# Masked attention over 4096 nodes on one core: the scores of a pair as seven half-size products instead of eight

## What is computed

```python
h = relu(layernorm(x))                     # x: 4096 x 512
q, k, v = h @ W_q.T + b_q, h @ W_k.T + b_k, h @ W_v.T + b_v
z = (q @ k.T) / sqrt(512)                  # 4096 x 4096
z = z * adj                                # adj: 0 or 1, 4096 x 4096
z = where(z == 0, -10000, z)
out = x + relu(softmax(z, axis=1) @ v)
```

## Time and profile before

| | us |
|---|---|
| median of 3 runs | 1589.69 (1583.79 to 1591.4) |
| the profiled execution | 1589.79 |
| its span | 1588.0 |
| PE busy, share of span | 1559.6, 98% |
| DVE busy | 1121.8, 71% |
| ACT busy | 554.0, 35% |
| transfers | 254.20 MB, mean 160 GB/s |

### The profile page before, as it was taken

The page is one execution under the profiler, slowest core; times in us unless marked ns, Lnnn a source line. Parts: engine busy times, 40 slices in busy tenths (PEclk is TensorE's granted clock), DMA queues, the critical chain, the costliest instruction groups (busy, mean ns, idle before and its releaser), DMA issues.

```text
span 1588.0 us, 18704 instructions
## 1 busy us (share of the span) xinstructions
PE 1559.6 (98%) x7246; PEld 721.8 (45%) x7246; DVE 1121.8 (71%) x1306; ACT 554.0 (35%) x666; POOL 2.3 (0%) x11
## 2 busy tenths in 40 slices
PE   7899999899999999999999999999999999999998
PEld 3344444344444444444444444444444444444444
DVE  5766764478776877687767776777767776777675
ACT  1233332243334333433334332433343333333342
POOL 0000000000000000000000000000000000000000
PEclk9899999999999999999999999999999999999999
DMA  4344325464544554455345533554435543453241
GB/s 165 120 145 160 133 106 184 162 227 171 184 160 153 182 184 158 159 186 187 145 158 185 206 142 144 185 192 173 142 143 211 186 153 128 171 199 120 67 160 67
DMA packets 75320, 254.20 MB, mean 160 GB/s; under 512 B 8288, under 2 KB 8288, under 8 KB 73440
## 3 DMA queue, kind: packets, MB, share of 16 engines
q1 hardware_dynamic: 75232, 253.00, 44.5%
HBM read 220.47 MB, written 32.51 MB: 159 GB/s over the span
## 4 chain that ended last, share of the span: by engine, by line
PE 95%; DVE 2%; issue 0%; ACT 0%; DVEq 0%; ACTq 0%
PE z L437 42%; PE o L452 42%; PE o L398 5%; PE o L412 5%; PE o L380 1%; PE z L483 0%; PE z L464 0%; PE z L474 0%; DVE o_rows L863 0%; DVE dot_waste L752 0%; DVE slots L885 0%; DVE stats L711 0%; DVE slots L790 0%; DVE run_min L802 0%; DVE acc L744 0%
## 5 line engine op out<-in xcount | busy, mean ns | idle before, releaser
L437 PE MATMUL z<-h_buf,g_buf 128*128 128x512 f16 x3072 | 683.8, 379 | 0.0
L452 PE MATMUL o<-v_buf,p_hi 128*128 128x512 f16 x2048 | 610.1, 380 | 0.4 <-issue 0.4
L437 PEld LDWEIGHTS z<-h_buf,g_buf 128*128 128x128 f16 x3072 | 300.7, 98 | 362.6 <-issue 1.1
L452 PE MATMUL o<-v_buf,p_lo 128*128 128x512 f16 x1024 | 388.6, 379 | 0.0
L785 DVE TENSOR_TENSOR slots<-slots,adj_buf 128x512 f32<-128x512 f32 x256 | 176.2, 691 | 283.4 <-ACT slots L592 283.2
L598 ACT ACTIVATE slots<-slots,log_p 128x1024 f32<-128x1024 f32 x128 | 147.2, 1150 | 474.4 <-DVE slots L822 474.4
L452 PEld LDWEIGHTS o<-v_buf,p_hi 128*128 128x128 f16 x2048 | 200.7, 98 | 237.9 <-issue 2.1
L592 ACT ACTIVATE slots<-z,c_all,kappa 128x512 f32<-128x512 f32 x256 | 198.9, 777 | 289.8 <-PE z L437 263.9
L829 DVE TENSOR_TENSOR p_lo<-slots,p_hi 128x1024 f16<-128x1024 f32 x128 | 156.6, 1224 | 45.0 <-PE o L452 30.0
L822 DVE TENSOR_TENSOR slots<-slots,floor_b 128x1024 f32<-128x1024 f32 x128 | 155.3, 1219 | 13.8 <-ACT floor_b L611 10.3
L790 DVE SCALAR_TENSOR_TENSOR slots<-slots 128x1024 f32<-128x1024 f32 x128 | 156.6, 1223 | 3.7
(11 more groups left out here) (89 smaller groups left out, 378.4 us busy)
## 6 DMA issues: line engine op xcount, KB each, us to landing
adj_buf<-in_adj SPq DMA_DIRECT2D x128, 512.0 KB, 5.6
v_buf<-v_dram SPq DMA_DIRECT2D x128, 512.0 KB, 3.7
g_buf<-g_dram SPq DMA_DIRECT2D x112, 512.0 KB, 4.6
x_rows<-in_x SPq DMA_DIRECT2D x12, 1024.0 KB, 8.0
v_dram<-v_buf SPq DMA_DIRECT2D x16, 512.0 KB, 7.5
g_dram<-g_buf SPq DMA_DIRECT2D x16, 512.0 KB, 8.0
h_dram<-h_buf SPq DMA_DIRECT2D x7, 1024.0 KB, 6.5
h_buf<-h_dram SPq DMA_DIRECT2D x7, 1024.0 KB, 8.2
```

What stands on the lines that cost most here:

```text
L437: mm = pe.matmul(z_bank[i % 2][t][:, :], g_buf[:, i % G_BUFS, a, k, t * P:(t + 1) * P], h[:, b, k, :], start=(k == 0 and m == 0), stop=(k ...
L452: mm = pe.matmul(o_bank[t][:, :], a[:, kt, span], v_buf[:, n % V_BUFS, kt, b, :], start=(j == 0 and kt == 0 and m == 0), stop=(j == PAIRS ...
```

## The change

- **Seven products.** `scores(i, piece)` splits the folded keys of a pair into 2 x 2 blocks (two key tiles by two halves of the contraction) and the block of h into 2 x 2 (two halves of the contraction by two halves of the queries). The four blocks of the scores come from seven block products (the Strassen scheme in Winograd's form) instead of eight. Each product has 2 chunks x 3 = 6 matmuls of 128x256, so a step has 42 of 128x256 where it had 24 of 128x512.
- **Sums.** The key-side sums S1 to S4 are made once, in the opening stage (`combine_g`), and stored beside the keys: a pair of g has seven operands (`OPS`) instead of four chunk pairs, 896 KB instead of 512 KB for each load. The query-side sums T1 to T4 are made for every block (`combine_t`, `high_t`, `low_t`), in steps 7 to 12 of the block two before.
- **PSUM.** Products are added in the banks `za0`/`za1`, `zb`, `zd`, and read out between products: ACT makes seven copies of 128x256 per step instead of two of 128x512. TensorE's pieces wait for these (`m1_copied`, `u2_copied`, `m7_copied`, `u4_copied`, and the next pair for `m2_copied`, `d_copied`, `c12_copied`). DVE adds the copies (`add_c11`, `add_c2`); `weigh` is one instruction of 128x1024 instead of two.
- **Order.** In the main loop the pieces of `scores` stand between the four `weigh_v`. `LEAD` is 19 and there are 20 slots; g and v have 3 buffers instead of 4.
- **Opening.** `normalise` moves from DVE to ACT, DVE does the sums and splits seven operands. The next chunk of folded keys waits only for ACT's copy to `g_stage` (`g_copied`). Three pairs of the second block, instead of two, are scored ahead of step 0.
- Bias and x are handled in other steps, x comes back in halves, and several buffers share memory.

```diff
-        g_buf = sb("g_buf", [P, G_BUFS, 2, KC, 2 * P], F16)
+        g_buf = sb("g_buf", [P, G_BUFS, 2, OPS, 2, P], F16)
...
+            def product(i, bank, op, right, fresh):
+                for j in range(2):
+                    for m, (a, b) in enumerate(HI_LO):
+                        mm = pe.matmul(bank[:, 0:QH], g_of(i)[:, a, op, j, :], right[b][j],
+                                       start=(fresh and j == 0 and m == 0), stop=(j == 1 and m == 2),
+                                       skip_group_check=not fresh)
+                return mm
...
+                    product(i, a, A11, of_h(s, 0, 0), True).then_inc(za_ready, 1)
+                    if i >= 1:
+                        pe.wait_ge(m2_copied, i)
+                    product(i, b_bank, A12, of_h(s, 1, 0), True).then_inc(zb_ready, 1)
+                if piece == 1:
+                    if j == 0:
+                        pe.wait_ge(t_lo_ready, KC * (s + 1))
+                    pe.wait_ge(m1_copied, i + 1)
+                    product(i, a, S2, of_t(s, T2), False).then_inc(za_ready, 1)
+                    if i >= 1:
+                        pe.wait_ge(d_copied, i)
+                    product(i, d_bank, S3, of_t(s, T3), True).then_inc(zd_ready, 1)
+                if piece == 2:
+                    pe.wait_ge(u2_copied, i + 1)
+                    product(i, a, S1, of_t(s, T1), False).then_inc(za_ready, 1)
+                    pe.wait_ge(m7_copied, i + 1)
+                    product(i, d_bank, A22, of_t(s, T4), False).then_inc(zd_ready, 1)
+                if piece == 3:
+                    pe.wait_ge(u4_copied, i + 1)
+                    product(i, a, S4, of_h(s, 1, 1), False).then_inc(za_ready, 1)
...
+            def copy_u2(i):
+                act.wait_ge(za_ready, 4 * i + 2)
+                if i >= 1:
+                    act.wait_ge(c2_added, i)
+                nc.scalar.activation(um_tmp[:, 0, :], a_bank[i % 2][:, 0:QH], ACT.Identity, bias=key_term(i, 1),
+                                     scale=kappa[:, 0:1]).then_inc(u2_copied, 1)
...
+            def low_g(q, j):
+                for u in range(2):
+                    g = g_of(2 * q + u)
+                    dve.wait_ge(g_hi_ready, 4 * q + 2 * j + u + 1)
+                    v.tensor_tensor(g[:, 1, :, j, :], g_stage[:, 0:OPS, u, :], g[:, 0, :, j, :], ALU.subtract
+                                    ).then_inc(g_lo_ready, 1)
...
+            def add_c2(i):
...
+                v.tensor_tensor(slot(i)[:, 1, :], um_tmp[:, :, :].rearrange("p a n -> p (a n)"),
+                                dm_tmp[:, :, :].rearrange("p a n -> p (a n)"), ALU.add).then_inc(c2_added, 1)
```

More of the change, by code:

```diff
@@ L658, in _ @@
[L658 to L667 removed]
+            normalise(4)
@@ new lines, in _ @@
+            for n in range(-3, STEPS):
+                s, j = n // PAIRS, n % PAIRS
+                first = j == PAIRS - 2 and 0 < s + 1 < BLOCKS
+                more = n + LEAD < STEPS
+                soon = 2 <= n + 2 < STEPS
+                if PAIRS <= n + LEAD - 1 < STEPS:
+                    copy_c12(n + LEAD - 1)
+                if j == 0 and s >= 1:
+                    copy_o(s - 1, 3)
+                if more:
+                    copy_m1(n + LEAD)
+                    copy_m2(n + LEAD)
+                if soon and not first:
+                    exp(n + 2)
+                if more:
+                    copy_u2(n + LEAD)
+                    copy_m7(n + LEAD)
+                if first:
+                    copy_floor(s + 1, a_bank[0])
+                if n == -1:
+                    copy_floor(0, o_bank[3])
+                if soon and not first:
+                    high_p(n + 2)
+                if s >= 0 and s + 2 < BLOCKS:
+                    if j == 9:
+                        high_t(s + 2, 0)
+                    if j == 10:
+                        high_t(s + 2, 1)
+                        high_t(s + 2, 2)
+                    if j == 11:
+                        high_t(s + 2, 3)
+                if more:
+                    copy_u4(n + LEAD)
+                    copy_d(n + LEAD)
+                if n == -1:
+                    exp(0)
+                    high_p(0)
+                    exp(1)
+                    high_p(1)
+                if first:
@@ new lines, in _ @@
+            add_c11(PAIRS)
+            add_c2(PAIRS)
+            halve_min(0)
+            weigh(PAIRS)
+            add_c11(PAIRS + 1)
+            negate(PAIRS)
+            see_min(PAIRS)
+            add_c2(PAIRS + 1)
+            columns_min(0, o_bank[2])
+            weigh(PAIRS + 1)
+            add_c11(PAIRS + 2)
+            negate(PAIRS + 1)
+            lower(0)
+            add_c2(PAIRS + 2)
+            lower(1)
+            see_min(PAIRS + 1)
+            low_p(0)
+            for n in range(STEPS):
+                s, j = n // PAIRS, n % PAIRS
+                first = j == PAIRS - 2 and s + 1 < BLOCKS
@@ L988, in _ @@
                 i = n + LEAD
-                if n + 2 < STEPS and not first:
+                more, scored = i < STEPS, i - 1 < STEPS
+                if first:
+                    halve_min(s + 1)
+                elif n + 2 < STEPS:
                     lower(n + 2)
-                if 0 <= n + 1 < STEPS:
+                if scored:
+                    weigh(i - 1)
+                if n + 1 < STEPS:
                     low_p(n + 1)
-                    add_up(n + 1)
-                if first:
-                    halve_min(s)
@@ L1011, in _ @@
-                if j == 0 and s >= 1:
-                    halve_acc(s - 1)
+                if j == PAIRS - 1:
+                    row_gain(s)
+                if first:
+                    columns_min(s + 1, a_bank[0])
+                if scored:
+                    negate(i - 1)
+                if n + 1 < STEPS:
+                    add_up(n + 1)
+                if j == PAIRS - 2:
+                    halve_acc(s)
+                if more:
+                    add_c11(i)
+                if s >= 1 and j in (1, 3):
+                    add_bias(s - 1, j - 1, j + 1)
```

910 lines of the change are left out of this document (557 added, 353 removed).

## The result

| | before | after |
|---|---|---|
| median, us | 1588.34 (1583.79 to 1591.4, 4 runs) | 1533.72 (1532.2 to 1534.65, 4 runs) |
| ratio, 95% interval | | 0.9657 (0.9631 to 0.9683) |
| span of the profiled execution | 1588.0 | 1532.8 |

The account below looks back on a forecast made before the run. TensorE's streamed columns were taken as the bound. 1588.0 - 76.8 (scores) - 4 (start) + 8 and + 5 (opening rounds) + 3.5 (block ends) = 1523.7 us, plus 1.8 outside the span: 1526 forecast, range 1506 to 1562.

Parts of the forecast that it names:

- TensorE's work: Scores of a step: 42 short matmuls at 109 ns, step 9.76 us instead of 10.36, 76.8 us saved over 128 pairs.
- the bound from the transposes: Price of a 256-column matmul: float32 128x128 transposes start every 109 ns, so short matmuls were put at 109 ns.
- Hand-offs in the main loop: ScalarE's copies between score pieces: priced at nothing under six long matmuls (1.3 us); uncovered, 0.5 to 1 us each a step.
- the line between two rows: ScalarE's 128x256 copies, interpolated from 4-column and 512-column instructions: 0.49 us with a key term, 0.45 without.
- VectorE: Main loop: about 9.1 us of work in a 9.76 us step, 93%; it fits, narrowly.
- the prediction's check on the kernel before: VectorE's step before the change, by the same count: 7.35 + 7.3/16 = 7.8 us where the stretch shows 7.5.
- slower than before: Main-loop rival: VectorE sets the step through lower, exp, u2, add_c2 once past 10.36 us; 1636 us, chance 0.05.
- Block ends: End-of-block chain through lower, exp and high_p delays the next step: 0.5 us for each of 7, +3.5 us.
- the start: Opening before the first values: normalise moved to ScalarE saves between 0 and 8 us, taken as -4.
- query sums of the first block in round 1: nothing: Opening round 1: VectorE about 23 us beside TensorE's 22.5, so no cost.
- Rounds 2 to 7: Opening: VectorE fits, but the keys' chain is 1 to 1.5 us late in some 8 rounds, +8 us (0 to 16).
- Rounds 8 and 9: Opening's end with three extra pairs: same 56 us expected, part of the counted gain lost, +5 us (0 to 12).

Follow-up runs that it names:

- e3: Changed kernel with the four score pieces in one run ahead of the values in 14 of 16 steps; 1682.78 us, ratio 1.0585.
- e4: Changed kernel with ScalarE's normalise and square_root behind the score copies of their part, in the opening only; 1522.96 us, ratio 0.9583.
- e7: e4 plus, in opening rounds 2 to 7, values ahead of a part's first scores and the next piece behind the folded keys; 1519.88 us, ratio 0.9579.
- e1: Kernel before with each 128x512 score matmul issued as two of 128x256, each with its own weight load; 1595.96 us, ratio 1.0039.
- e2: Kernel before with each score matmul issued as four of 128x128; 1609.25 us, ratio 1.0123.

## Why the prediction was right, and where it was not

- **TensorE's work: right.** 42 starts of 109 ns, a step of 9.77 us where 9.76 was forecast. The width alone costs what the bound from the transposes said (7.2 us for 8), and the weight loads never show. The sentence of the Trainium skill on overlap ("TensorE: Matmul & The Clock Gate", packing small matmuls, The mechanism) does not hold here, not even at 128 columns, where 56 ns pass between loads of 98 ns. The same section also lets a load into the background weight buffer pass ahead, which the prediction left out; the runs do not show which buffer the loads went to. The 107 ns that the LDWEIGHTS section of that page gives for 128 columns are near the 98 ns of the record as a duration, but loads follow each other every 56 ns.
- **Hand-offs in the main loop: right, priced at nothing,** and the stretch shows no wait. Without the cover, 0.5 to 1 us was said for each; e3 shows 0.17, 0.74 and 0.45 us, 1.36 a step, and is slower than the kernel before. ScalarE's copies took 0.56 and 0.47 us where the line between two rows gave 0.49 and 0.45, so its step is 5.9 us and not 5.5; the cover of 1.3 us held even so.
- **VectorE: right in kind.** 8.5 us a step where I had 9.1. A part of the 0.6 is a slip: five instructions of 1.22 and two of 0.69 are 7.5 us, not the 7.35 of the prediction's check on the kernel before, so the overlap was taken too small. Its limit is the mean, not the worst step. The rival "slower than before" was a real one with two instructions of room: at about 10.8 us of work on VectorE the kernel is 5% slower than before.
- **Block ends: wrong in sign.** +3.5 us was forecast. The main part shrank by 68.5 us; 109 pairs of 0.595 and the 1.3 us of scores moved ahead of it make 66.2, so the block ends and the tail cost 2.3 us less than before, and the 0.5 us at each of seven block ends do not show. The prediction read the main loop of the kernel before as free of gaps, but its last block end has one, followed by matmuls at the lower clock; the changed kernel waits nowhere between 366 and 1430 us:

```profile
1486.38 0.99 PE L464 MATMUL z<-ident,half_min 128*128 128x128 f32 x4 [1.96 <-DVE half_min L806]
```

- **Opening: the start was right at first, then given back.** The first keys start at 63.48 instead of 67.54 us, 4.1 us earlier (4 forecast), with the same matmuls done before them; e4 shows that the order of ScalarE's list had held back another 4.0. But by the second part of round 2 TensorE is 1.3 us late (93.90 against 92.60). The step "query sums of the first block in round 1: nothing" failed: from the first keys to there 30.4 us pass instead of 25.1, a loss of 5.4. Of it, 1.7 us are the values at 79.06, which wait for `low_v` behind VectorE's query sums, statistics and key-side sums. Another 1.9 are the values at 86.88, where `low_v` waits for ScalarE's `high_v`, queued behind a `normalise` that itself waits for VectorE; and 1.4 are the first scores, on `low_g`:

```profile
79.06 2.75 PE L475 MATMUL o<-slots,h_buf 128*128 128x512 f16 x12 [1.58 <-DVE v_buf L1013]
...
86.88 2.75 PE L475 MATMUL o<-slots,h_buf 128*128 128x512 f16 x12 [1.76 <-DVE v_buf L1013]
...
93.90 0.83 PE L502 MATMUL za<-h_buf,g_buf 128*128 128x256 f16 x6 [1.24 <-DVE g_buf L1033]
```

No run moved the query sums of the first block, so what they cost alone is not shown. e4 takes the second wait away and still needs 30.55 us, because the first is longer there and is followed by matmuls at the lower clock.
- **Rounds 2 to 7: mis-sized.** +8 was forecast, 16 measured (201.2 us to the second part of round 8, where the 192.3 of before less 7.1 for 12 pairs make 185.2). The failed step is that sum of the rounds, which held the chain of the keys alone. That chain is there, at 1.55 us a round (1 to 1.5 said); e7 removed it. What I had missed is ScalarE's list: `normalise` and `square_root` ahead of the score copies, 2.5 us in each of rounds 3 to 5, which e4 removed. These three rounds make 12.3 of the 16 us. VectorE was not the bound: 26.5 us a round in e7, where about 28 was said. I had counted `normalise` as freed VectorE time and never asked what was queued behind it on its new engine.
- **Rounds 8 and 9: right,** +6.0 for +5. The longest wait, 4.4 us, is the last keys' chain with some of VectorE's backlog; the next, 3.27 us, is the one ahead of the first values.
- The sum closes: 1588.0 - 76.2 (128 x 0.595) + 1.3 + 16.0 + 6.0 - 2.3 = 1532.8. Forecast for the same terms was 1523.7; the opening cost 14 us more than forecast (5.3 at the start and in round 1, 8 in rounds 2 to 7, 1 at its end), and the block ends 6 us less. So the total is nearer its forecast than its terms are, by luck.

## What to carry to other kernels

A scheme that trades columns for more products is worth its columns only if other matmuls lie over the read-out of each product; here 1.3 us of them were enough, and with none the scheme lost more than it saved. Place them first, then count. When an instruction moves to another engine, look at what it waits for and what is queued behind it there: here two kinds of cheap instruction, ahead of copies that TensorE needs, cost 11 us. And load the second engine on purpose once: one and two added instructions bracket its room, which its busy share alone does not.

## What the runs showed of the hardware

- Matmuls of 512, 256 and 128 columns start every 215.8, 109 and 56 ns, each with a new load of 128x128 float16 weights whose record is 98 ns long: the columns at 2.4 GHz and 2.5 ns, at all three (e1, e2 and both kernels).
- After some waits TensorE runs at its lower level (1.2 GHz) for a while. The kernel after, behind a wait of 4.4 us; from 319.7 to 322.2 us the granted clock is 0.50, and a matmul of 256 columns starts every 213 ns:

```profile
318.65 1.24 PE L502 MATMUL za<-h_buf,g_buf 128*128 128x256 f16 x6 [4.41 <-DVE spare L1033]
319.69 1.49 PE L502 MATMUL zb<-h_buf,g_buf 128*128 128x256 f16 x6
320.97 1.49 PE L502 MATMUL za<-h_buf,g_buf 128*128 128x256 f16 x6
322.25 0.87 PE L502 MATMUL zd<-h_buf,g_buf 128*128 128x256 f16 x6
```

Three runs of six take 3.60 us instead of 1.97, so the wait of 4.4 us cost 6.0. The waits of 0.6 to 1.5 us in the rounds before had no such tail. The length of the wait alone does not decide it: the same wait of 2.17 us had a tail in e4 (first row) and none in e7 (second row). I had not priced this.

```profile
75.63 4.43 PE L475 MATMUL o<-slots,h_buf 128*128 128x512 f16 x12 [2.17 <-DVE v_buf L1009]
```

```profile
77.31 2.75 PE L475 MATMUL o<-slots,h_buf 128*128 128x512 f16 x12 [2.17 <-DVE v_buf L1024]
```
